# Modulation products read their condition columns 32 times over, and all five engines get new orders for the first and last iterations of a four-stage transformer kernel

## What is computed

```
m = silu(mod) @ w_ada + b_ada          # 9 vectors of 256 for each batch: shift, scale, gate x 3
h = _ln(x) * (1 + sc_msa) + sh_msa
x = x + _self_attn(h, ...) * g_msa     # stage A: windows of 128 rows, 16 heads of 16
h = _ln(x) * (1 + sc_mca) + sh_mca
x = x + _topk_cross_attn(h, context, ...) * g_mca   # stage B: only the 16 largest of 77 scores of a row count
h = _ln(x) * (1 + sc_mlp) + sh_mlp
x = x + _swiglu(h, ...) * g_mlp        # stage C: hidden width 1024
# stage D: cross attention of a second block, its scale and bias from silu(c) @ W_ss for x and for the context
x = x_q + (softmax(q k / sqrt(dh)) v) @ Wp + bp
```

## Time and profile before

| | us |
|---|---|
| median of 3 runs | 980.44 |
| lowest and highest run | 979.55, 982.67 |
| the profiled execution | 981.46 |
| its span, first to last instruction | 979.7 |

### The profile page before, as it was taken

One profiled execution on the slowest core, in us unless ns is written; L12 is line 12 of the kernel. 1 busy time (PEld: TensorE's weight loads), 2 busy tenths in 40 slices (PEclk: granted clock), 3 DMA queues, 4 the chain that ended last, 5 costly groups with the idle time before them and its releaser, 6 DMA issues. The chain is left out here.

```text
span 979.7 us, 32584 instructions
## 1 busy us (share of the span) xinstructions
PE 932.0 (95%) x10500; PEld 809.7 (83%) x10500; DVE 868.1 (89%) x4318; ACT 744.6 (76%) x1604; POOL 701.1 (72%) x1099
## 2 busy tenths in 40 slices
PE   6987899999999999999999999999999999998996
PEld 3775788888888898888888888888888898777884
DVE  2569999999999999999999999999999999897633
ACT  2355788888878888888888888888888887687764
POOL 1226867887777788787777778878777777666752
PEclk9779999999999999999999999999999999999998
DMA  8276200123333332223333333222333333210000
GB/s 289 62 150 135 67 18 18 26 65 77 72 73 76 77 78 51 63 64 68 77 71 72 77 77 73 46 68 65 71 78 70 73 78 71 46 33 7 7 7 18
DMA packets 210555, 66.44 MB, mean 68 GB/s; under 512 B 188520, under 2 KB 200961, under 8 KB 209746
## 3 DMA queue, kind: packets, MB, share of 16 engines
q1 hardware_dynamic: 210386, 64.35, 29.6%
HBM read 39.02 MB, written 25.30 MB: 66 GB/s over the span
## 5 line engine op out<-in xcount | busy, mean ns | idle before, releaser
L2344 PE MATMUL ps<-hT_C,w_m_sb 128*128 128x128 f32 x2048 | 256.6, 278 | 1.9 <-DVE hidden_C L1674 1.5
L2344 PEld LDWEIGHTS ps<-hT_C,w_m_sb 128*128 128x128 f32 x2048 | 243.6, 192 | 14.4 <-issue 8.2
L1043 ACT ACTIVATE silu_C<-ps,cols_sb 128x128 f32<-128x128 f32 x256 | 93.6, 366 | 121.8 <-PE ps L2344 109.9
L2355 PE MATMUL ps<-w_m_sb,hidden_C 128*128 128x256 f32 x512 | 121.1, 380 | 0.2
L1580 DVE MATCH_REPLACE8 scores_left_B<-mx_B,scores_left_B 128x77 f32<-128x77 f32 x512 | 108.3, 224 | 0.0
L1576 DVE MATCH_REPLACE8 scores_left_B<-mx_B,scores_B 128x77 f32<-128x77 f32 x512 | 108.1, 224 | 0.0
L2355 PEld LDWEIGHTS ps<-w_m_sb,hidden_C 128*128 128x128 f32 x512 | 92.7, 190 | 10.9 <-DVE hidden_C L1674 0.7
L666 POOL TENSOR_TENSOR scores_D<-scores_D,mx_D 128x616 f32<-128x616 f32 x62 | 76.0, 1226 | 25.0 <-DVE mx_D L1647 24.9
L661 POOL TENSOR_TENSOR p_B<-scores_B,mx_B 128x616 f32<-128x616 f32 x64 | 78.5, 1227 | 19.6 <-DVE mx_B L1574 19.0
L1674 DVE SCALAR_TENSOR_TENSOR hidden_C<-ps,cols_sb,silu_C 128x128 f32<-128x128 f32 x256 | 83.6, 337 | 9.7 <-ACT silu_C L1043 9.5
L701 POOL TENSOR_TENSOR p_D<-scores_D,rc_D 128x616 f32<-128x616 f32 x63 | 77.0, 1225 | 10.9 <-DVE rc_D L1625 5.4
(11 more groups left out here) (188 smaller groups left out, 2439.7 us busy)
## 6 DMA issues: line engine op xcount, KB each, us to landing
p_turned_D<-p_blocks_D SPq DMA_DIRECT2D x200, 80.0 KB, 2.4
pT_D<-p_turned_D SPq DMA_DIRECT2D x50, 320.0 KB, 3.5
xn_turned_A<-xn_blocks_A SPq DMA_DIRECT2D x124, 32.0 KB, 2.0
xn_A<-xn_turned_A SPq DMA_DIRECT2D x31, 128.0 KB, 2.1
x_A<-in_x SPq DMA_DIRECT2D x28, 128.0 KB, 2.4
out<-y_D SPq DMA_DIRECT2D x28, 128.0 KB, 2.1
w_m_sb<-in_w_m SPq DMA_DIRECT2D x3, 1024.0 KB, 5.2
w_mod_sb<-in_w_mod SPq DMA_DIRECT2D x2, 1024.0 KB, 9.9
```

What stands on the lines that cost most here:

```text
L1043: sc.activation(SA[:, j, :], bank(f"C.up{j}")[:, 0:P], ACT.Silu, bias=col("bm1_a", j)).then_inc(sa_ok, 1)
L2344: ins = mm(bank(f"C.up{j}")[:, half * P:(half + 1) * P], w_m1[:, k, m:m + P], HT["C"][:, t % HT_COPIES["C"], k, :], start=(k == 0), stop=( ...
L2355: ins = mm(bank("C.dn0")[:, 0:CH], G[:, t % G_COPIES, j, :], w_m2[:, j, :], start=(j == 0), stop=(j == HJ - 1))
```

## The change

The computation stays the same. On PE, the 4 condition columns are read 32 times over, so that 128 columns stream through each block of weights in place of 4; the 32 copies of each result land side by side in PSUM, where one product now takes 128 columns in place of 4. VectorE reads the first copy alone. Each of the 40 products is as before in number and in weights.

```
@@ block.vector, set_up_modulation(ln)
-                mod = ps[:, ln % 2, 0:16].rearrange("p (m i b) -> p m i b", m=2, b=BATCH)
+                mod = ps[:, ln % 2, :].rearrange("p (m i r b) -> p m i r b", m=2, i=KC, b=BATCH)[:, :, :, 0, :]
@@ block.tensor, set_up_modulation(ln)
                 for i in range(4 * ln, 4 * ln + 4):
                     for c in range(KC):
-                        ins = mm(ps[:, ln % 2, i % 4 * BATCH:(i % 4 + 1) * BATCH], w_mod[:, c, i * P:(i + 1) * P], scT[:, c, :],
-                                 start=(c == 0), stop=(c == KC - 1))
+                        ins = mm(ps[:, ln % 2, i % 4 * P:(i % 4 + 1) * P].rearrange("p (r b) -> p r b", b=BATCH), w_mod[:, c, i * P:(i + 1) * P],
+                                 scT[:, c, :].unsqueeze(1).to_broadcast([P, P // BATCH, BATCH]), start=(c == 0), stop=(c == KC - 1))
@@ block.tensor, fill()
+                set_up_modulation(0)
                 transpose_h(0, "A")
-                set_up_modulation(0)
+                project_q(0, "A")
                 set_up_gates()
-                project_q(0, "A")
```

More of the change, by code:

```diff
@@ L1069, in fill @@
-                queries(2, "A")
                 set_up_context()
-                normalise(3, "A")
+                exponentials(0, "B", 0)
                 key_blocks(2)
+                set_up_values("D")
+                normalise(1, "B")
+                modulate(3, "A")
+                normalise(4, "A")
+                set_up_keys("D")
+                top_exponentials(0)
+                modulate(1, "B")
                 values(2)
-                top_exponentials(0)
-                exponentials(0, "B", 0)
@@ L1109, in fill @@
                 exponentials_a(3, 1)
                 output_t(1, "B")
+                exponentials(2, "B", 0)
                 silu(0, 0)
@@ L1156, in fill @@
                 exponentials(3, "B", 0)
+                exponentials(0, "D", 0)
+                top_exponentials(3)
                 normalise(4, "B")
@@ L1720, in fill @@
+                select(0, 0, 2)
                 select(0, 2, 1)
+                turn_outputs(1)
+                turn_back(1)
+                residual(1, "A")
+                statistics(4, "A")
+                select(0, 1, 1)
+                select(0, 2, 2)
                 select(0, 3, 1)
-                select(0, 0, 2)
+                statistics(1, "B")
                 select(0, 3, 2)
-                turn_outputs(1)
-                select(0, 2, 2)
+                select(0, 1, 2)
                 select(0, 1, 3)
-                turn_back(1)
@@ L1741, in fill @@
+                turn_input(4, "A")
                 add_maxima(2)
                 select(1, 0, 0)
+                select(1, 1, 0)
+                select(1, 3, 0)
+                select(1, 0, 1)
                 select(1, 2, 0)
-                select(1, 3, 0)
+                select(1, 1, 1)
                 select(1, 2, 1)
-                select(1, 0, 1)
-                select(1, 1, 0)
+                select(1, 0, 2)
+                select(1, 1, 2)
+                turn_outputs(2)
                 select(1, 3, 1)
+                turn_back(2)
@@ L1749, in fill @@
                 select(1, 2, 2)
-                select(1, 1, 1)
-                turn_outputs(2)
                 select(1, 3, 2)
-                select(1, 1, 2)
+                residual(2, "A")
+                select(1, 0, 3)
+                statistics(2, "B")
                 residual(0, "B")
-                turn_back(2)
-                select(1, 3, 3)
-                select(1, 0, 2)
-                residual(2, "A")
+                select(1, 1, 3)
+                row_sums(1, "B")
                 statistics(0, "C")
-                statistics(2, "B")
@@ L1953, in drain @@
-                select(TILES - 3, 1, 2)
                 turn_input(TILES - 1, "A")
                 select(TILES - 3, 0, 1)
+                select(TILES - 3, 1, 0)
+                select(TILES - 3, 2, 0)
+                select(TILES - 3, 1, 1)
+                select(TILES - 3, 2, 1)
+                select(TILES - 3, 0, 2)
+                row_sums(TILES - 7, "D")
+                turn_outputs(TILES - 2)
+                select(TILES - 3, 3, 0)
+                hidden(TILES - 5, 0)
+                hidden(TILES - 5, 1)
@@ L1956, in drain @@
                 turn_weights(TILES - 7, "D", 0)
+                residual(TILES - 4, "B")
+                turn_back(TILES - 2)
+                hidden(TILES - 5, 2)
+                statistics(TILES - 4, "C")
                 turn_weights(TILES - 7, "D", 1)
-                select(TILES - 3, 2, 0)
-                turn_outputs(TILES - 2)
-                hidden(TILES - 5, 0)
-                select(TILES - 3, 2, 1)
+                hidden(TILES - 5, 3)
                 maxima_d(TILES - 6, 0)
-                select(TILES - 3, 0, 2)
@@ L2380, in fill @@
                 transpose_h(0, "B")
+                project_v(1)
                 project_q(0, "B")
@@ L2462, in fill @@
                 up(1, 7)
+                down(1, 0)
+                project_k(5)
+                down(1, 1)
                 project_q(5, "A")
-                project_k(5)
-                down(1, 0)
-                down(1, 1)
+                project_v(5)
                 transpose_h(4, "B")
+                scores_a(5)
                 transpose_h(2, "C")
-                scores_a(5)
-                project_v(5)
                 project_q(4, "B")
@@ L2504, in fill @@
                 project_v(6)
-                transpose_h(3, "C")
                 project_o(0, "D")
```

696 lines of the change are left out of this document (336 added, 360 removed).

## The result

The changed kernel takes 970.91 us (median of 4 runs, 970.15 to 972.71) where the kernel before takes 980.0 on the same chip: a ratio of 0.990, 95% interval 0.988 to 0.992. The profiled execution took 972.71 us, its span is 970.9.

A forecast was written before the change was run, and what follows sets the result against it. PE bounds the body, DVE close behind, so only the time before about 110 us and behind 810 us can change. 981.46 - 7.0 (fill) - 2 (drain) = 972.5 us profiled, 1.0 less for the median: 971.5 us, range 963 to 980.

The forecast's parts named there:

- the fill: Everything before PE is full at 110 us: 7.0 us gained in all, bounds 0 to 13.
- the drain: The last iterations, behind about 810 us: new orders gain 2 us, range -6 to +6.
- The clock: PE from 24.86 us to tile 0's scores: 128 columns keep 2.4 GHz, shortening PE's queue by 0 to 10.4 us.
- Rival 1: Modulation steps early on PE: the clock falls all the same, 978 to 980 us; chance 0.12.
- Start: First modulation step moved ahead of a waiting transpose: `scores_a(0)` 1.0 us sooner than 24.86 us, bounds 0 and 2.2.
- The chain to the first selection: Tile 0 through five engines up to VectorE's first selection at 61.24 us: 5.8 us sooner, the start's 1.0 included.
- rival 2: VectorE's in-order wait for `x_A` of tile 3 delays tile 0's outputs: slower, 983 us; chance 0.08.
- Behind the first selection: VectorE, full from there on, keeps its lead; `w_out_B` moved ahead, less later flat values: 1.2 us gained.
- The body: From 210 to 810 us: bound by PE, iteration still 27.3 us, the lead carried to its end.
- Last iterations: Behind about 810 us: new orders gain 2 us; idle times allow at most about 12.5 us.
- Rival 3: The new orders of the last iterations cost 6 us and more: 979 to 986 us; chance 0.08.
- Rival 4: More than forecast: fill gains 10 to 13 us, or drain gives 6: 960 to 966 us; chance 0.15.

The follow-up runs named there:

- e1: The kernel before with the 128 columns alone, all orders as before: 979.7 us, ratio 0.998.
- e2: The changed kernel with 4 columns again, all new orders kept: 975.3 us, ratio 0.994.
- e10: The changed kernel itself, run again on the chip of e9: 971.29 us, ratio 0.9883.
- e5: The changed kernel with SP's write and read of stage B's flat values moved ahead: 971.2 us, ratio 0.9905.
- e3: The changed kernel with the old orders of the last iterations on all five engines: 980.0 us, ratio 0.9978.
- e9: The changed kernel with SP's flat values of stage B and its load of tile 4 both moved ahead: 965.67 us, ratio 0.9829.
- e4: The kernel before with only the new orders of the last iterations, on all five engines: 974.1 us, ratio 0.993.
- e7: The kernel before with PE's new order of the last iterations alone: 988.0 us, ratio 1.0071.
- e6: The kernel before with VectorE's new order of the last iterations alone: 984.3 us, ratio 1.0035.
- e11: The kernel before with the new orders of the last iterations on VectorE and PE only: 985.4 us, ratio 1.0032.

## Why the prediction was right, and where it was not

The predicted 971.5 us meets 970.91, and that it does so closely is luck: two of its terms are wrong and cancel. It had 7.0 us for the fill and 2 for the drain; measured are about 2 and 7. The mechanism of the clock was right, what becomes of its gain was not.

- **The clock.** Right. 1.00 from 25 to 63 us, and it follows the columns, not the orders (e1, e2). Rival 1 is refuted for this stretch. Modulation steps take 2.02 to 2.05 us in place of 1.92 to 1.95, so the price of the columns was 0.1 us for each and not the 0.2 that I took.
- **Start.** Open by one trace. `scores_a(0)` is at 21.90 us, 3.0 and not 1.0 us sooner and above my bound of 2.2, and so it is in e10 (22.18) and e5 (21.74). But e3 and e9, whose PE program is the same up to there, have 23.93 and 23.72 us: 0.9 and 1.1 us sooner, as forecast. The first step, priced at 4.2 us, took 3.42 to 3.78. What differs is when PE comes to its full pace (see the last section), for which my sum had no term. It hardly matters: the first selection is at 53.46 and 53.25 us in e3 and e9, and between 52.57 and 53.30 in the others.
- **The chain to the first selection.** 7.9 us sooner where I took 5.8, inside the bounds, and 8 us in the mean of six old and five new fills. VectorE turned tile 0's outputs back at 41.53 us, as forecast (42), and its wait for `x_A` of tile 3 was 0.98 us, so rival 2 did not happen. With 128 columns the orders had no part in it that can be told: e1 has the same 53 us without them.
- **Behind the first selection.** This is the step that failed: "DVE, full from there on, keeps what it is ahead". I had read a busy 47.4 of 50 us as a bound, and it was one only as long as the transfers were early enough. With everything 8 us sooner the next waits are for SP: 5.18 us in e1, 4.53 in the changed kernel, 3.77 in e5. I had named the later flat values and priced them, with the gain of `w_out_B`, at a net gain of 1.2 us. Of 7.9 us 1.9 were left at tile 7 (2.5 by the means of six old and three new fills), and e9, with tile 7 at 201.51 us, shows that the better part of the loss lay in SP's order.
- **The body.** Right: (807.71 - 206.93) / 22 = 27.3 us, and the lead is carried through to within 0.5 us.
- **Last iterations.** The other term that failed, beyond its own bound of 6: 7.3 us by the drain's length in the two profiled executions, 7 by e4's median. The ceiling of 12.5 us that I read from the idle times wasn't exceeded; I then took 2, "nearer to nothing", with no row that said so. PE's last two body iterations went from 30.1 and 30.65 to 27.8 and 27.9 us, which is 5.0 of the 6.1 that I had counted as over, and the rest came behind them. Which wait the new orders remove there isn't shown. Rival 3 is refuted for the five orders together; PE's order alone (e7) costs the 7 us that it feared, and e6 and e11 cost about 3.
- **The rivals' numbers.** Rival 4's condition, a drain that gives 6 us or more, came true, but not its 960 to 966 us, since the fill gave 2 us and not 7. By its own terms rival 1 comes to 977 us (980.4 less 1, 1.2 and 2, plus about 1) and not to 978 to 980, and a chance of 0.11 for slower has room for 0.03 of rival 3's 0.08, which isn't most of it. Neither changes the forecast.

## What to carry to other kernels

When an edit makes engines faster ahead of a stretch that looks bound by one of them, look next at the transfers: list what SP starts there, when, and who waits, since its order was good enough only for the old pace. An order of one engine has no worth by itself where all of them run in order: the same PE order cost 7 us with the old neighbours and gave about 3 with the new ones, so a gain has to be looked for, and tested, over all queues at once. And split a measured gain by milestones of both traces before believing that the reason was right, even where the total is.

## What the hardware showed that was not expected

- A clock is lost in at least two ways here. Behind 4-column products it falls to 0.5 with PE busy for 3.4 of 4 us (e2, 24 to 28 us), and with 128 columns for the same products it doesn't fall between 24 and 64 us in any of six traces, at 0.1 us a step. With an idle stretch it falls too: in e1 PE has no product from 68 to 72 us, the clock falls near 71 us and is at 0.50 until 80 us. The Trainium skill, "TensorE: Matmul & The Clock Gate", section "HAM oscillation — how this bites in real kernels", tells of the second way alone; the trace of e1 agrees with it, and the modulation steps are outside of it. A third fall fits neither: in the changed kernel the clock goes to 0.5 from 77 to 79 us, where PE had been busy for 6.5 of the 10 us up to 76 us and idle for 1.93 us at most at a time. What set it off is open.
- At the start the granted clock and the durations disagree. PEclk reads 1.00 from the first microsecond on in both kernels, but the transposes and queries take twice as long in some executions as in others. PE's timeline of e2, to be set beside that of the changed kernel above:

```profile
5.35 3.58 PE L2136 MATMUL ps<-scT,w_mod_sb 128*128 128x4 f32 x16 [5.35 <-ACT scT L1409]
8.79 0.67 PE L2204 MATMUL ps<-ident_sb,xn_A 128*128 128x128 f32 x2
10.35 2.08 PE L2215 MATMUL ps<-hT_A,w_qkv_sb 128*128 128x128 f32 x8 [0.90 <-ACT hT_A L953]
12.36 3.80 PE L2146 MATMUL ps<-w_gate_sb,scT 128*4 128x512 f32 x8
```

0.67 against 0.38, 2.08 against 1.16, 3.80 against 2.74 us. It looks as if the 128 columns of the first step brought PE to its full pace sooner, but e3, which has them and the same program, is as slow as e2:

```profile
10.61 2.08 PE L2215 MATMUL ps<-hT_A,w_qkv_sb 128*128 128x128 f32 x8 [0.90 <-ACT hT_A L953]
12.62 3.79 PE L2146 MATMUL ps<-w_gate_sb,scT 128*4 128x512 f32 x8
```

So is e9 (2.08 and 3.72 us), while e5 and e10 are like the changed kernel (1.16 and 2.74 us). The pace of the first 16 us thus varies from execution to execution, and two traces can't tell what an edit does to it. That the column shows no 0.5 there means that early stretches are to be read by durations.
- Six executions of one and the same fill, that of the kernel before, put tile 7 between 207.4 and 212.1 us; three with 128 columns and the new orders between 206.3 and 207.1. The gates at the start vary with them, from 4.24 us (before) to 5.28 (e4, e11). Why the old fill varies more was not looked into.
